# First attention: inverse row sums by logarithm, exponential and a Newton step; GpSimd adds whole tiles; positions changed

## The reference, cut to what matters

```python
dots = jnp.einsum('bhnd,bhmd->bhnm', q, k) * scale      # 512 x 512 per head and batch
attn = jax.nn.softmax(dots, axis=-1)
out  = jnp.einsum('bhnm,bhmd->bhnd', attn, v)
out  = transpose(out).reshape(b, n, HEADS * DIM_HEAD) @ w_out + b_out
```

## Time and profile before

| | value |
|---|---|
| profiled execution, span | 3025.9 us, its own time is this span |
| median of three timed runs | 3018.5 us |
| PE, DVE, ACT, POOL busy | 92%, 70%, 57%, 58% of the span |
| granted TensorE clock, mean | 0.956 |
| first attention, about | 250 to 1380 us |
| second attention, about | 1850 to 2800 us |

### The profile page before, as it was taken

How to read it: one execution, slowest core, us unless ns; L and a number is a source line. 1 busy time by engine, 2 the same in 40 slices (tenths; PEclk the granted TensorE clock), 3 DMA queues, 4 the chain that set the end, 5 groups by cost and what they waited for, 6 DMA issues and landing times. The chain is left out here.

```text
span 3025.9 us, 50008 instructions
## 1 busy us (share of the span) xinstructions
PE 2770.4 (92%) x17716; PEld 1938.1 (64%) x17716; DVE 2107.9 (70%) x4508; ACT 1731.9 (57%) x3340; POOL 1752.1 (58%) x1540
## 2 busy tenths in 40 slices
PE   7999999999999999989994787999999999999376
PEld 6995565656656565648883674666666666665276
DVE  5667777777777777666776435877877778777632
ACT  5665777776776767676772343544544545445142
POOL 0004989898898989891110573555555555555067
PEclk9999999999999999989996798999999999999588
DMA  3015444444544545420002331000000000000033
GB/s 101 1 58 129 119 117 117 115 114 109 130 106 113 123 106 131 105 71 5 23 15 67 72 60 33 2 5 5 9 5 6 5 9 5 5 6 9 28 84 50
DMA packets 146695, 179.65 MB, mean 59 GB/s; under 512 B 31571, under 2 KB 76176, under 8 KB 145936
## 3 DMA queue, kind: packets, MB, share of 16 engines
q1 hardware_dynamic: 132368, 165.72, 21.7%
q0 software_dynamic: 14080, 10.73, 2.7%
HBM read 56.51 MB, written 17.72 MB: 25 GB/s over the span
## 5 line engine op out<-in xcount | busy, mean ns | idle before, releaser
L1982 POOL TENSOR_TENSOR arena<-arena 128x512 f32<-128x512 f32 x1152 | 1447.0, 1284 | 565.7 <-ACT arena L1325 450.8
L1605 DVE TENSOR_REDUCE top<-psum 128x1 f32<-128x512 f32 x1536 | 974.6, 677 | 196.0 <-PE psum L917 123.6
L1325 ACT ACTIVATE arena<-psum 128x512 f32<-128x512 f32 x1536 | 840.8, 600 | 240.7 <-PE psum L917 141.3
L909 PE MATMUL psum<-stack 96*128 96x512 f32 (+1 forms) x2048 | 627.5, 426 | 16.5 <-ACT arena L1325 9.3
L960 PE MATMUL psum<-arena,values 128*32 128x512 f32 (+1 forms) x3072 | 477.6, 597 | 3.4 <-ACT arena L1325 3.4
L909 PEld LDWEIGHTS psum<-stack 96*128 96x128 f32 (+1 forms) x2048 | 344.0, 191 | 198.1 <-DVE top L1605 87.7
L960 PEld LDWEIGHTS psum<-arena,values 128*32 128x32 f32 (+1 forms) x3072 | 134.0, 119 | 290.0 <-issue 284.8
L917 PE MATMUL psum<-stack 64*128 64x512 f32 x2048 | 292.5, 399 | 11.8 <-DVE top L1605 5.6
L1951 POOL TENSOR_SCALAR rstd<-mv 128x4 f32<-128x4 f32 x56 | 13.0, 233 | 480.0 <-DVE mv L1466 478.1
L1636 DVE RECIPROCAL psum<-psum 128x128 f32<-128x128 f32 x256 | 228.5, 934 | 25.3 <-PE psum L999 25.3
L917 PEld LDWEIGHTS psum<-stack 64*128 64x128 f32 x2048 | 200.4, 184 | 59.0 <-issue 26.0
(11 more groups left out here) (189 smaller groups left out, 3895.3 us busy)
## 6 DMA issues: line engine op xcount, KB each, us to landing
stack<-halves SPq DMA_DIRECT2D x768, 128.0 KB, 2.3
qk_ring<-qk_split SPq DMA_DIRECT2D x64, 256.0 KB, 2.9
v_ring<-v_split SPq DMA_DIRECT2D x32, 256.0 KB, 3.0
tokens<-xn SPq DMA_DIRECT2D x16, 256.0 KB, 2.4
arena<-in_wg SPq DMA_DIRECT2D x16, 256.0 KB
arena<-in_wu SPq DMA_DIRECT2D x16, 256.0 KB
arena<-in_wd SPq DMA_DIRECT2D x16, 256.0 KB
wqkv<-in_w_qkv SPq DMA_DIRECT2D x2, 1536.0 KB, 9.5
```

Source lines behind the costliest of these rows:

```text
L909: return T_.matmul(bk, st[0:k, side, h, cols], st[0:k, 1 - side, h, :], start=True, stop=True)
L1325: S_.activation(prob[l][tile % N_PROB[l]][:, h, :], psum[:, bank[key], :], ACT.Exp, scale=scale).then_inc(released[bank[key]], 1)
L1605: give(V_.reduce_max(top[i][:, column:column + 1], psum[:, bank[key], :], AX.X), key)
L1982: ins = G_.tensor_tensor(to[:, h, :], old[:, h, :], prob[l][tile % N_PROB[l]][:, h, :], ALU.add)
```

## The change

In `mix` of the first attention the two transposes, the small reciprocal and the spreading go. ScalarE takes the logarithm of `dn` and then exp(-x), which gives a near inverse r in `inverse`. VectorE makes dn * r in the bank, then (dn * r - 2) * r in `inverse`, and last `weighted` * -1 * `inverse` into `mixed`. `dn` is now held until the second VectorE step. The four calls of `mix` lie between 3.940 and 3.954. On VectorE the order is: product in the bank, Newton step, `ml` of `rows`, last product. ScalarE loads the table set that holds both functions in rounds 0, 62 and 63. GpSimd adds a whole tile in one instruction, 128x2048 in the first attention, 128x1024 in the second. The starts and ends of `project`, `maxima`, `probs`, `last`, `mix` and `ahead` of the first attention move; those of the second do not.

```diff
-    dict(project=(-0.11, 0.70), maxima=(0.98, 1.84), rows=(1.95, 1.95), probs=(2.25, 3.17), last=(3.25, 3.37),
-         mix=(3.94, 4.55), out=(4.53, 5.01), ahead=(-2.31, -0.79), finish=(4.91, 4.91), settle=(5.57, 5.86)),
+    dict(project=(-0.092, 0.718), maxima=(1.027, 1.840), rows=(1.950, 1.950), probs=(2.294, 3.170),
+         last=(3.312, 3.312), mix=(3.940, 3.954), out=(4.530, 5.010), ahead=(-2.284, -0.764),
+         finish=(4.910, 4.910), settle=(5.570, 5.860)),
@@ program_order
-            queue("mix", (l, n), 5, 5, n)
+            queue("mix", (l, n), 5 if l else 4, 5 if l else 4, n)
@@ tensor: mix, with its two turns, is gone
@@ scalar: mix
-                S_.activation(r, psum[:, bank[key], :], ACT.Copy).then_inc(released[bank[key]], 1)
...
-                S_.activation(r.rearrange("p (t h w) -> p t h w", t=TILES_B, h=HEADS[l]),
-                              recips[n % 2][:, :, :].unsqueeze(3).to_broadcast([P, TILES_B, HEADS[l], WIDTH[l]]),
-                              ACT.Copy).then_inc(spread, 1)
+                if n == 0 or n + 2 >= N_GROUPS:
+                    S_.preload_act_table_set("natural_log_exp_and_others")
+                S_.activation(near, psum[:, bank[key], :], ACT.Ln).then_inc(logged, 1)
+                act.wait_ge(logged, n + 1)
+                S_.activation(near, near, ACT.Exp, scale=-1.0).then_inc(inverse_near, 1)
@@ vector: mix
-                    give(V_.reciprocal(recips[i][:, :, :], psum[:, bank[turned], :].rearrange(
-                        "p (t h w) -> p t h w", t=TILES_B, h=HEADS[l])[:, :, :, 0]), turned)
...
+                    dve.wait_ge(inverse_near, n + 1)
+                    done = tick(V_.tensor_tensor(dn, dn, inverse[i], ALU.mult))
                     yield
+                    dve.wait_ge(*done)
+                    done = give(V_.scalar_tensor_tensor(out=inverse[i], in0=dn, scalar=2.0, in1=inverse[i],
+                                                        op0=ALU.subtract, op1=ALU.mult), key)
...
-                    give(V_.tensor_tensor(mixed[l][:, g, :], weighted[l][i], psum[:, bank[back], :], ALU.mult), back)
+                    V_.scalar_tensor_tensor(out=mixed[l][:, g, :], in0=weighted[l][i], scalar=-1.0, in1=inverse[i],
+                                            op0=ALU.mult, op1=ALU.mult).then_inc(divided0, 1)
@@ gpsimd: probabilities
-                        for h in range(heads):
-                            ins = G_.tensor_tensor(to[:, h, :], old[:, h, :], prob[l][tile % N_PROB[l]][:, h, :], ALU.add)
-                        ins.then_inc(summed, 1)
+                        G_.tensor_tensor(to, old, prob[l][tile % N_PROB[l]], ALU.add).then_inc(summed, 1)
```

More of the change, by code:

```diff
@@ L34 @@
 WHEN = (
-    dict(project=(-0.11, 0.70), maxima=(0.98, 1.84), rows=(1.95, 1.95), probs=(2.25, 3.17), last=(3.25, 3.37),
-         mix=(3.94, 4.55), out=(4.53, 5.01), ahead=(-2.31, -0.79), finish=(4.91, 4.91), settle=(5.57, 5.86)),
-    dict(rows=(1.82, 1.82), queries=(0.75, 0.75), keys=(0.80, 0.80), values=(1.01, 1.01), maxima=(1.04, 1.48),
-         probs=(3.03, 3.47), last=(3.43, 4.05), sums=(4.38, 4.38), mix=(4.38, 4.83), out=(4.93, 4.97),
-         ahead=(-1.52, 0.45), route=(5.03, 10.53), ranks=(9.80, 10.86), keep=(10.00, 10.00)))
+    dict(project=(-0.092, 0.718), maxima=(1.027, 1.840), rows=(1.950, 1.950), probs=(2.294, 3.170),
+         last=(3.312, 3.312), mix=(3.940, 3.954), out=(4.530, 5.010), ahead=(-2.284, -0.764),
+         finish=(4.910, 4.910), settle=(5.570, 5.860)),
+    dict(rows=(1.820, 1.820), queries=(0.750, 0.750), keys=(0.800, 0.800), values=(1.010, 1.010),
+         maxima=(1.040, 1.480), probs=(3.030, 3.470), last=(3.430, 4.050), sums=(4.380, 4.380), mix=(4.380, 4.830),
+         out=(4.930, 4.970), ahead=(-1.520, 0.450), route=(5.030, 10.530), ranks=(9.800, 10.860),
+         keep=(10.000, 10.000)))
 EXPERT_ROUNDS = 1.6
@@ L323, in mix @@
     def mix(self, l, n):
-        dn, turned, back = ("dn", l, n), ("turned", l, n), ("back", l, n)
+        for _ in range(TILES_B if l else 2):
+            yield
+        self.other.give(("dn", l, n))
+        yield
         if l == 0:
[L326 to L339, removed]
             yield
@@ L499, in build @@
         ml = [sb(f"ml{i}", [16, P], f32r) for i in range(2)]
-        recips = [sb(f"recips{i}", [P, TILES_B, 4]) for i in range(2)]
         y = sb("y", [P, TILES_B, DIM])
@@ L636, in build @@
         max_high = sem("max_high")
-        spread = sem("spread")
+        logged, inverse_near, divided0 = sem("logged"), sem("inverse_near"), sem("divided0")
         logits_exp = sem("logits_exp")
@@ L746, in divided @@
         def divided(l, n):
-            return read(("dn" if l else "back", l, n))
+            return read(("dn", l, n)) if l else (divided0, n + 1)
         def last_of_slot(n_slots, slot):
@@ L1002, in sums_of @@
                 yield
[L1004 to L1017, removed]
             def project_out(l, b):
@@ L1137, in _ @@
             play(order, dict(prepare0=prepare0, route=route, ahead=ahead, compute0=compute0, project=project,
-                             maxima=maxima, rows=rows_of_maxima, probs=probabilities, last=last_tiles, sums=sums_of, mix=mix,
+                             maxima=maxima, rows=rows_of_maxima, probs=probabilities, last=last_tiles, sums=sums_of,
                              out=project_out, fold=fold, experts1=experts1))
@@ L1344, in mix @@
                     return
-                r = inverse[n % 2]
-                key = ("dn", l, n)
+                near, key = inverse[n % 2], ("dn", l, n)
                 if n >= 2:
-                    act.wait_ge(*written(("back", l, n - 2)))
+                    act.wait_ge(*divided(l, n - 2))
                 act.wait_ge(*written(key))
-                S_.activation(r, psum[:, bank[key], :], ACT.Copy).then_inc(released[bank[key]], 1)
[L1351 to L1354, removed]
-                S_.activation(r.rearrange("p (t h w) -> p t h w", t=TILES_B, h=HEADS[l]),
-                              recips[n % 2][:, :, :].unsqueeze(3).to_broadcast([P, TILES_B, HEADS[l], WIDTH[l]]),
-                              ACT.Copy).then_inc(spread, 1)
+                if n == 0 or n + 2 >= N_GROUPS:
[3 more added lines that the diff above has]
+                S_.activation(near, near, ACT.Exp, scale=-1.0).then_inc(inverse_near, 1)
                 yield
@@ L1620, in mix @@
                 i, key = n % 2, ("dn", l, n)
+                dn = psum[:, bank[key], :]
                 if l == 0:
-                    turned = ("turned", l, n)
                     yield
+                    dve.wait_ge(inverse_near, n + 1)
+                    done = tick(V_.tensor_tensor(dn, dn, inverse[i], ALU.mult))
                     yield
-                    if n >= 2:
-                        dve.wait_ge(spread, n - 1)
-                    dve.wait_ge(*written(turned))
-                    give(V_.reciprocal(recips[i][:, :, :], psum[:, bank[turned], :].rearrange(
-                        "p (t h w) -> p t h w", t=TILES_B, h=HEADS[l])[:, :, :, 0]), turned)
-                    yield
+                    dve.wait_ge(*done)
+                    done = give(V_.scalar_tensor_tensor(out=inverse[i], in0=dn, scalar=2.0, in1=inverse[i],
+                                                        op0=ALU.subtract, op1=ALU.mult), key)
                     yield
@@ L1642, in mix @@
                 dve.wait_ge(*read(("o", l, n)))
+                dve.wait_ge(*done)
                 if l == 0:
-                    back = ("back", l, n)
-                    dve.wait_ge(*written(back))
-                    give(V_.tensor_tensor(mixed[l][:, g, :], weighted[l][i], psum[:, bank[back], :], ALU.mult), back)
-                else:
-                    dve.wait_ge(*done)
-                    give(V_.tensor_tensor(mixed[l][:, g, :], weighted[l][i], psum[:, bank[key], :], ALU.mult), key)
+                    V_.scalar_tensor_tensor(out=mixed[l][:, g, :], in0=weighted[l][i], scalar=-1.0, in1=inverse[i],
+                                            op0=ALU.mult, op1=ALU.mult).then_inc(divided0, 1)
+                else:
+                    give(V_.tensor_tensor(mixed[l][:, g, :], weighted[l][i], dn, ALU.mult), key)
                 yield
```

## The result

The changed kernel took 3234.31 us (median of 4 runs, 3233.76 to 3235.95) against 3018.86 us before on the same chip: 1.0719 times as long, 95% interval 1.0704 to 1.0734. The profiled execution has a span of 3231.9 us, 206 us more than before. The forecast was 3160 us with a range of 2992 to 3215 us; the measured time lies above it. The profiled execution before was itself longer than the median of its timed runs, which is why the medians lie 215 us apart and the profiled spans 206.

A forecast was written before the change was run, and what follows sets the result against it. No single engine bounded it, but a round loop of four engines, VectorE's maxima delaying TensorE. Blocked rounds +126, `out` rounds +5, second attention +8, tables +2 make +141 on 3025.9, 3167, less 7.4: 3160 us, range 2992 to 3215.

The forecast's parts named there:

- the mechanism and the sign: First attention: the last product, with two SBUF inputs, waits 3.0 us for GpSimd's addition; kernel slower, chance 0.69.
- A+6.15: First attention's round: last product ready 6.15 us after A, the start of the first GpSimd addition.
- A+9.75: First attention's round: last product ends 9.75 us after A, the first addition's start, having waited for the second.
- The four extra table loads: ScalarE: three forced table loads of 1.28 us and reloads they cause, bounds 0 to 8 us, taken as 2.
- the size of one term: First attention, after the blocked product: VectorE sets the pace, 10.45 us to the last maximum, giving an 18.5 us round.
- a rival at 0.08: GpSimd's 2048-column instruction no cheaper than four, or clock falling to 1.2 GHz in TensorE's pauses: +205, 3224 us; chance 0.08.
- the count: First attention: 56 of 64 rounds blocked, each 2.25 us longer, the same phase each round: +126 us.
- The second attention: Additions of 2.38 us make L1492 wait up to 1.1 us longer, six times, and L1761 some tenths: +8 us.
- The moved places: First attention's moved starts and ends: no order that matters changes, costed at 0, bounds -45 to +45 us.
- The rival that no wait matters: First attention: block short, in a pause or absorbed; rounds 15.5 to 16.4 us, -22 us, 2996 us; chance 0.22.
- the forecast of +141: Whole kernel: all terms together add 141 us to the profiled 3025.9 us, giving 3167, predicted as 3160 us.

The follow-up runs named there:

- e1: Changed kernel with the Newton step's result left in the bank, so the last product reads one SBUF input instead of two: 3031.08 us, 1.0020 of before.
- e3: Kernel before with whole-tile GpSimd additions in both attentions, nothing else of the change: 3043.57 us, 1.0056 of before.
- e4: Changed kernel with the last product alone moved from 3.9505 to 4.60, into GpSimd's pause: 3055.62 us, 1.0093 of before.
- e2: Changed kernel with one head per GpSimd addition in both attentions, the product keeping two SBUF inputs: 3031.60 us, 1.0022 of before.
- e6: Changed kernel with two heads per GpSimd addition in both attentions: 3083.09 us, 1.0193 of before.
- e5: Changed kernel with ten more, overwritten TensorE products before the fourth score of rounds 1 to 62: 3198.60 us, 1.0572 of before.
- e11: e9 with project, maxima, probs, last and ahead of the first attention at their old places: 3047.11 us, 1.0074 of before.
- e9: e1 with one head per GpSimd addition in the second attention alone, whole tiles in the first: 3015.36 us, 0.9963 of before.
- e7: Changed kernel with project, maxima, probs, last and ahead of the first attention at their old places: 3324.52 us, 1.0982 of before.
- e8: e1 with one head per GpSimd addition in both attentions: 3017.98 us, 0.9976 of before.

## Why the prediction was right or wrong

**Right, the mechanism and the sign.** The last product waits for the addition under way and gets in before the next: predicted ready at A+6.15, it was at A+5.81; predicted end A+9.75, found A+9.85; additions predicted 4.57 us, found 4.59 in the mean where no product contends (e1, e3). The four extra table loads (24 of 1.28 us instead of 20) are 5 us at most, inside the bounds of 0 to 8. e1 removes the wait and e4 dodges it. e2 and e6 shorten it with GpSimd's instruction.

**Wrong, the size of one term.** "It regains nothing, since from then on VectorE sets the pace: 16 maxima at 0.61 and one low half (0.69) are 10.45 us to the last maximum". It took 12.46 us from the first maximum (861.19) to the end of the last (873.65). With the others as found, 9.78 + 12.46 - 1.64 = 20.60 us, the measured round, against 18.5. VectorE did not set the pace all the way: it idled 1.80 us for TensorE, whose weighing ran at the 1.2 GHz level. With the clock held (e5) the term is 892.54 - 881.77 = 10.77 us and the round 18.97, so 1.6 of the 2.1 us missing are the clock; the other 0.5 us were not traced further. I had named a falling clock in half a sentence of a rival at 0.08, and priced it at the upper end of something else; it belonged into the sum, because the forecast itself made TensorE stand for about 3 us in each blocked round.

**Wrong and hidden, the count.** I took 56 blocked rounds at 2.25 us, since "the phase is the same each round"; it was about 48 of 64, six of a batch's eight, and a blocked round is 4.3 us above 16.25. 48 x 4.3 = 206, about the measured 200. The seventh regular round of a batch escapes by GpSimd's four small instructions, which I had not looked for (read from the timeline; no run moves them). So the count was too high and the round too short, and the two misses partly cancelled: 48 rounds at my 2.25 us would have been 108 us instead of 126.

**The second attention**: +8 predicted, +17 found. L1492 was right at 1.08 us more; L1761 I called "some tenths", it was 1.41 in the median: in three of seven cases it was issued 0.08 us after an addition had begun and took 2.32 us, where before it came 0.7 us into an addition of 1.28 and took 0.59.

**The moved places** were costed at 0, with -45 to +45 us around it, since I found no order that they change and that mattered. They are worth -34 us without the wait (e11 against e9), inside those bounds, and -80 beside it (e7 against after), outside them. Without them the change is 9.8% slower, 297 us, and against that the forecast of +141 misses by more than it does against the change as it is.

**The rival that no wait matters** stood at 2970 to 3028 us, middle 2996. That state exists as e1: 3031, less the 17 us of the second attention that the rival didn't have, less 6 us for another chip, on which the kernel before took that much longer, about 3008. Its rounds of 16.1 us lie inside the 15.5 to 16.4 named there. What failed in that rival was its condition; its price of -22 us was near, with -11 found.

## What to carry to other kernels

Before giving a VectorE instruction a second SBUF input, or GpSimd a longer one, look whether they meet: the waiting counts as busy time, so find it in a line's minimum, median and maximum, not in the idle column. The cure may be one operand in PSUM, or a place in the queue where the other engine rests. When a forecast makes TensorE stand for a few us in each round, price the work behind the pause at half the clock too, and when a step moves, search the places around it anew.

## What the runs showed of the hardware that I had not expected

- A pause of 2.96 us in each round of 20.6 was followed by some 3.4 us at 1.2 GHz (0.50 in the windows), beginning between 863 and 864, after TensorE had resumed at 861.92. Where the median wait was 1.3 us (e6) and 0.5 (e2), the mean clock over 400 to 1300 us stayed at 0.99; with the long waits it was 0.94, in e7 0.90, and with the pause filled in e5 1.00.
- GpSimd pays as well, but little. The three additions of a blocked round take 14.26 us where they take 14.04 in e4, and the one that takes longer is the third, which starts at 860.86 while the product still runs until 861.26 and lasts 4.81 us. In the mean it is 4.636 us after against 4.588 where no product contends (e3), and in e2 1.301 against 1.283 (e8).
- A waiting VectorE instruction gets in between two additions that are both queued: every waiting product of the changed kernel ended 0.55 us after the addition that it had met, and the waits follow the length of one addition (longest product 1.77, 2.65 and 4.68 us beside 1.30, 2.42 and 4.64), not of three.
